# Two small powers on GpSimd behind every second row transfer of the scatters

## The chip, the cores and the metric

The kernel runs on one core of one Trainium2 chip. The metric is the device time of one execution in microseconds (us): the median of three runs before the change is 1126.06 us (1124.15 to 1128.71).

## The reference

Eight sequences of 512 tokens of 128 values pass through two layers. Each layer is an attention and a feed-forward part with experts, each behind a layer norm and with a residual.

```python
x = x + _L0_attn_ref(_layernorm(x), ...)   # 16 heads of 8, 4 key/value heads, causal
x = x + _L0_ffn_ref(_layernorm(x), ...)    # 8 experts, the best one a token, silu(a) * g @ w2
x = x + _L1_attn_ref(_layernorm(x), ...)   # keys and values from a latent of 32, rotary positions, causal
x = x + _L1_ffn_ref(_layernorm(x), ...)    # 8 experts, the best two a token, relu(x w1 + b1) w2 + b2
```

## The kernel before

**Attention.** The work goes batch by batch (8 batches of 512 tokens) through both layers. For each batch TensorE first makes scores for the row maxima, in units of up to 512 columns by two banks (L1354, L1360), and VectorE reduces them (`neg_max`, L1658). GpSimd computes the lowest part of the split maxima (`max_parts`, L1220), SyncE stores it and loads it back into the query stack (L1079, L1085). Then TensorE makes the transposed scores (L1380), ScalarE the exponentials (`scratch`, L1588), GpSimd sets the part above the diagonal to zero (`affine_select` on `scratch`, L1230, four a quad of heads), and TensorE multiplies with the values (`psum<-scratch,values`, L1398), which ScalarE copies out (`ctx_raw`, L1484). GpSimd has further small steps: four operations of the layer norm's statistics with one power (L1185 to L1190), the lowest parts of queries and keys (L1207), sums of the rotary products (L1212, L1216).

**Experts.** After four batches (a half, g = 0 or 1) VectorE chooses experts for 2048 tokens and computes, for each token, its row in a list sorted by expert (`rows_of`, L1866). GpSimd then scatters the normed rows (`xn_half`) to these places in device memory (`sorted_in`, L1241): one indirect DMA moves 128 rows, 16 of them a half in layer 0, and 2 x 16 a half in layer 1, where the second 16 (k = 1) of a batch wait for a mark that VectorE writes into the rows (`xn_half`, L1677) once the first 4 of the batch have landed. SyncE fetches the sorted rows in groups of four tiles (`rows_in`, L1130), the first group of a half once all scatters of the half have landed, and the weights of each tile's expert (`w_now`, L1116). TensorE transposes the rows (L1449) and computes the two products of each tile of 128 rows (L1466, L1476), with ScalarE (L1624) and VectorE (L1655) between. In layer 0 the results go to memory and come back by indirect gathers (L1258). In layer 1 GpSimd sends each tile back with an indirect DMA (`returned`, L1249), and SyncE takes the rows back at the end (L1150).

**Order.** Every engine has one fixed program. A table of times (`schedule`) gives each step a due time, and `Plan` walks it with costs per step and makes one order for each engine (`plan.order`). Attention of later batches and experts of a half are interleaved in these orders. An engine doesn't pass a step that waits. On GpSimd the scatters are steps of their own; those of layer 0 stand in one row, those of layer 1, half 0, stand among masks of the attention, and those of layer 1, half 1, stand among sends. Each waits only at its batch's first transfer:

```python
elif s.kind == "scatter":
    g, x, (t, k) = s.b, s.x, s.y
    if t == QT * x and k == 0:
        pool.wait_ge(placed, s.layer * HALVES + g + 1)
        pool.wait_ge(normed, of("norm", s.layer, g * GB + x, "half").n + 1)
        pool.wait_ge(filled[s.layer], FILLED[s.layer])
    if t == QT * x and k == 1:
        pool.wait_ge(marked, of("mark", 1, g, x).n + 1)
```

Of the kernel before, what the change touches and what calls it, by code (L numbers as in the profile page):

```python
# [8 lines left out]
ALU = mybir.AluOpType  # L9
# [5 lines left out]
QT = SEQ // P  # L15
# [48 lines left out]
C_ID, C_FIRST, C_ONE, C_RANK, C_THR, C_SLOT, C_HALF = 0, 128, 256, 264, 272, 288, 328  # L64
C_TOKEN = 332
C_EPS, C_MINUS = C_TOKEN + GT, C_TOKEN + GT + QT
# [37 lines left out]

TAKE_BEHIND = 14
DMA = 16

ROW = DIM + 1
RETURNED = 2 * GT * P
# [625 lines left out]
def two_layers(nc, d):  # L735
    with ExitStack() as ctx:
# [3 lines left out]
        def sem(name):  # L740
            return ctx.enter_context(nc.semaphore(name))
# [8 lines left out]
        consts = sb("consts", [P, C_ALL])  # L750
# [58 lines left out]
        r_small = sb("route_small", [P, 4, GT])  # L809
# [43 lines left out]
        route_exp, normed = sem("route_exp"), sem("normed")  # L853

        values_set, zeroed, lat_made = sem("values_set"), sem("zeroed"), sem("lat_made")
        rs_made, stats_made = sem("rs_made"), sem("stats_made")
        lat_scaled, lo_made, summed, max_lo, masked = sem("lat_scaled"), sem("lo_made"), sem("summed"), sem("max_lo"), sem("masked")

        rows_set = sems("rows_set", STACKS)
# [12 lines left out]

        REST_LOADED = REST_LOADS * DMA
        W2_LOADED = EXPERTS * DMA
        FILLED = [len(times) * DMA for times in FILLS]

# [15 lines left out]
        def parks_done(s):  # L892

            done = 0
            for k in range(stack_of(s), batch_of(s) + 1, STACKS):
                done += DMA * 3
            return done

        def stacks_done(name, k):

            return sum(4 * DMA if name == "k" and j < BATCHES else 2 * DMA for j in range(k % STACKS, k + 1, STACKS))

# [35 lines left out]
        def rows_sent(layer, g, x):  # L938

            return DMA * QT * (g + 1) if layer == 0 else DMA * QT * (HALVES + 2 * (g + 1))  # L940

# [228 lines left out]
        @block.gpsimd  # L1170
        def _(pool):
            for i in range(3):
                pool.memset(values[i][:, :, :], 0.0).then_inc(values_set, 1)
            for i in range(3):
                pool.wait_ge(values_set, 3)
                pool.memset(values_of(i, HEADS)[:, :, :, HD:VW], 1.0).then_inc(values_set, 1)
            pool.memset(gathered[0], 0.0).then_inc(zeroed, 1)
            pool.wait_ge(consts_loaded, 2 * DMA)
            for s in plan.order("pool"):
                if s.kind == "stats":  # L1180

                    mean, var, scale, shift = (ln_small[s.slot][:, :, x:x + 1] for x in range(6, 10))
                    pool.wait_ge(var_made, s.n + 1)
                    eps, half, minus = (consts[:, x:x + QT].unsqueeze(2) for x in (C_EPS, C_HALF, C_MINUS))
                    pool.tensor_tensor(scale, var, eps, ALU.add).then_inc(rs_made, 1)  # L1185
                    pool.tensor_tensor(shift, mean, minus, ALU.mult).then_inc(rs_made, 1)
                    pool.wait_ge(rs_made, 3 * s.n + 2)
                    pool.tensor_tensor(scale, scale, half, ALU.pow).then_inc(rs_made, 1)  # L1188
                    pool.wait_ge(rs_made, 3 * s.n + 3)
                    pool.tensor_tensor(shift, shift, scale, ALU.mult).then_inc(stats_made, 1)  # L1190

                elif s.kind == "norm":

                    b = s.b
                    out = lat_n[:, :, :]
                    pool.wait_ge(normed, s.n + 1)
                    pool.tensor_tensor(out, out, ln_gb[:, 0:1, :].to_broadcast([P, QT, LATENT]), ALU.mult).then_inc(lat_scaled, 1)
                    pool.wait_ge(lat_scaled, b + 1)
                    twice = [P, QT, 2, LATENT]
                    pool.tensor_tensor(lat_twice[:, :, :, :], out.unsqueeze(2).to_broadcast(twice), ln_gb[:, 1:2, :].unsqueeze(1).to_broadcast(twice),  # L1200
                                       ALU.add).then_inc(lat_made, 1)

                elif s.kind == "mid":
                    n = P if s.layer == 0 and s.x == "k" else SEQ
                    pool.wait_ge(mid_made, s.n + 1)
                    parts, rest = parts_of[s.x], rest_of[s.layer, s.x]
                    pool.tensor_tensor(parts[:, 2, 0:n], rest[:, 0:n], parts[:, 1, 0:n], ALU.subtract).then_inc(lo_made, 1)  # L1207

                elif s.kind == "sum":
                    u = (of("rotate", 1, s.b, "q", 1) if s.x == "q" else of("rotate_k", 1, s.b)).uses[0]  # L1210
                    pool.wait_ge(read[u.bank], u.after)
                    pool.tensor_tensor(exact[:, :], rot[0][:, :], rot[1][:, :], ALU.add).then_inc(summed, 1)  # L1212

                elif s.kind == "hi":
                    pool.wait_ge(hi_made, 2 * batch_of(s) + (s.x == "k") + 1)
                    pool.tensor_tensor(rest_of[1, s.x][:, :], exact[:, :], parts_of[s.x][:, 0, :], ALU.subtract).then_inc(rest_made, 1)  # L1216

                elif s.kind == "m_mid":
                    pool.wait_ge(max_mid, s.n + 1)
                    pool.tensor_tensor(max_parts[:, 2, :], max_rest[:, :], max_parts[:, 1, :], ALU.subtract).then_inc(max_lo, 1)  # L1220

                elif s.kind == "score":

                    u = s.uses[0]
                    pool.wait_ge(read[u.bank], u.after)
                    units, stride, offs = MASKS[s.y]
                    first = 2 * SEQ * (s.slot - units + 1)
                    for off in offs:
                        diag = scratch[:, first:first + 4 * stride].rearrange("p (x n) -> p x n", x=4)[:, :, off:off + P]
                        pool.affine_select(out=diag, in_=diag, compare_op=ALU.is_ge, fill=0.0, base=0, pattern=[[0, 4], [1, P]],  # L1230
                                           channel_multiplier=-1).then_inc(masked, 1)
# [8 lines that stand above are left out]
                        pool.wait_ge(marked, of("mark", 1, g, x).n + 1)  # L1240
                    pool.indirect_dma_start(sorted_in[s.layer][g][:, :], bass.IndirectOffsetOnAxis(ap=rows_of[g][k][:, t:t + 1], axis=0),  # L1241
                                            xn_half[:, t, 0:widths[s.layer]], None).then_inc(scattered[x], DMA)

                elif s.kind == "send":
                    g, slot = s.b, of("second", 1, s.b, s.x).slot
                    u = of("second", 1, g, s.x).uses[0]
                    pool.wait_ge(places_known, places_read(of("turn_rows", 1, g, s.x // 4)))
                    pool.wait_ge(read[u.bank], u.after)
                    pool.indirect_dma_start(returned[g][:, :], bass.IndirectOffsetOnAxis(ap=goes_to[g][:, s.x:s.x + 1], axis=0),  # L1249
                                            kept[slot], None).then_inc(sent_back[slot], DMA)  # L1250

                elif s.kind == "combine":
                    g, x, (t, k) = s.b, s.x, s.y
                    if t == QT * x and k == 0:
                        for slot, value in enumerate(stores_made(g)):
                            pool.wait_ge(stored[slot], value)
                    if s.n >= 4:
                        pool.wait_ge(combined, s.n - 3)  # L1258
                    pool.indirect_dma_start(gathered[s.slot], None, sorted_out[g][:, :],
                                            bass.IndirectOffsetOnAxis(ap=rows_of[g][k][:, t:t + 1], axis=0)).then_inc(gathered_in[s.slot], DMA)  # L1260

                elif s.kind == "add":
                    rows = X[:, s.b * GT + QT * s.x:s.b * GT + QT * s.x + QT, :]
                    pool.wait_ge(weighed, s.y + 1)
                    if s.y:
                        pool.wait_ge(added_apart, s.y)
                    pool.tensor_tensor(rows, rows, taken_back(s.b, s.x, s.y), ALU.add).then_inc(added_apart, 1)
# [706 lines left out]
```

## Time and profile before

| | |
|---|---|
| median of the timed runs | 1126.06 us |
| span of the profiled execution, first to last instruction | 1133.8 us |
| mean granted TensorE clock | 0.890 |
| TensorE busy | 920.3 us, 81% |
| VectorE busy | 649.8 us, 57% |
| ScalarE busy | 611.0 us, 54% |
| GpSimd busy | 516.6 us, 46% |
| scatters L1241 | 96, 92.7 us, mean 966 ns |
| sends L1249 | 78, 75.4 us, mean 966 ns |
| masks L1230 | 256, 159.4 us, mean 639 ns |
| powers of the statistics L1188 | 40, 41.2 us, mean 1030 ns |

The profile is of one execution. Its span, 1133.8 us, is what the page gives as that execution's own time; what lies around the span is not in it. Busy shares are means over stages that differ. An idle time is put down to the releaser that came last; "issue" is time in which the engine waited for nothing that the profile shows, and "remote" (in the chain "another core or an unknown queue") a wait whose end the trace can't put down to any engine. PEclk is the share of full clock that was granted to TensorE. Lines are those of the kernel before; a helper's line (L1655, L1658, L1484) serves many steps.

### The profile page before, as it was taken

The page shows a single profiled execution, that of the slowest core. Times are in us where ns is not written, and L with a number is a line of the kernel's source. Part 1 is how long each engine was busy: PE and PEld are TensorE (multiplying, and loading weights), DVE is VectorE, ACT ScalarE, POOL GpSimd, SP SyncE. Part 2 cuts the span into 40 slices and gives each one's busy share as a digit, 9 for nine tenths or more (in the row PEclk, how much of TensorE's full clock was granted, in tenths as well). Part 3 has the DMA queues.
Part 4 walks back from the last instruction along what each step waited for, and adds up shares of the span by engine and source line. Part 5 has one row for each costly group of instructions (what it writes and reads, how often), then busy time and mean ns, then how long its engine had stood idle before and what let it go on. Part 6 is the DMA issues. An engine that isn't in the chain of part 4 may idle for free.

```text
span 1133.8 us, 24903 instructions
## 1 busy us (share of the span) xinstructions
PE 920.3 (81%) x8964; PEld 605.2 (53%) x8964; DVE 649.8 (57%) x1266; ACT 611.0 (54%) x1170; POOL 516.6 (46%) x747
## 2 busy tenths in 40 slices
PE   4789889848998899975999789987689984788781
PEld 2344445415986445432897345533245774687771
DVE  1987988838434787785556787887455151011116
ACT  3277777702454766853544478763368752254451
POOL 3153443460013875556103775647744436615452
PEclk9999999967999887996999899996769996898896
DMA  6446233252763251452762445334311454466657
GB/s 165 109 126 182 66 88 74 74 158 60 231 204 105 73 149 70 89 155 63 219 200 87 91 139 136 88 86 138 80 37 33 127 150 119 141 184 174 174 160 233
DMA packets 136722, 142.75 MB, mean 126 GB/s; under 512 B 35036, under 2 KB 112924, under 8 KB 136444
## 3 DMA queue, kind: packets, MB, share of 16 engines
q1 hardware_dynamic: 130012, 127.61, 40.9%
q0 software_dynamic: 6592, 13.55, 3.7%
q8 instruction: 76, 1.25, 0.5%
q14 instruction: 42, 0.34, 0.1%
HBM read 100.32 MB, written 45.95 MB: 129 GB/s over the span
## 4 chain that ended last, share of the span: by engine, by line
PE 57%; DVE 12%; ACT 10%; another core or an unknown queue 9%; issue 6%; DMA 3%; POOL 2%; SPq 1%; DVEq 0%; ACTq 0%; POOLq 0%
PE psum L1466 13%; PE psum L1398 12%; PE psum L1476 9%; DVE neg_max L1658 8%; PE psum L1380 5%; ACT scratch L1588 5%; PE psum L1354 5%; PE psum L1424 2%; PE psum L1360 2%; ACT hidden_t L1624 2%; PE psum L1433 1%; PE psum L1286 1%; PE psum L1316 1%; PE psum L1408 1%
## 5 line engine op out<-in xcount | busy, mean ns | idle before, releaser
L1658 DVE TENSOR_REDUCE neg_max<-psum 128x2 f32<-128x768 f32 (+3 forms) x352 | 381.1, 1119 | 117.1 <-PE psum L1360 69.6
L1588 ACT ACTIVATE scratch<-psum 128x1024 f32<-128x1024 f32 x320 | 317.3, 1023 | 128.6 <-PE psum L1380 85.2
L1230 POOL TENSOR_SCALAR_AFFINE_SELECT scratch<-scratch 128x512 f32<-128x512 f32 x256 | 159.4, 639 | 309.1 <-ACT scratch L1588 308.5
L1398 PE MATMUL psum<-scratch,values 128*32 128x512 f32 (+3 forms) x2048 | 180.8, 479 | 3.5 <-POOL scratch L1230 3.0
L1354 PE MATMUL psum<-k_stack,q_stack 52*128 52x128 bf16 (+3 forms) x1024 | 140.3, 335 | 51.2 <-DVE neg_max L1658 23.7
L1466 PE MATMUL psum<-rows_t,w_now 128*128 128x128 f32 x1360 | 179.1, 284 | 1.9 <-issue 1.3
L1466 PEld LDWEIGHTS psum<-rows_t,w_now 128*128 128x128 f32 x1360 | 166.4, 198 | 9.0 <-issue 6.4
L1476 PE MATMUL psum<-w,hidden_t 128*128 x992 | 142.2, 290 | 34.7 <-ACT hidden_t L1624 19.8
L1380 PE MATMUL psum<-q_stack,k_stack 55*128 55x512 bf16 (+3 forms) x1024 | 129.0, 324 | 47.7 <-DVE neg_max L1658 19.1
L1476 PEld LDWEIGHTS psum<-w,hidden_t 128*128 128x128 f32 x992 | 127.8, 202 | 44.8 <-issue 44.6
L1624 ACT ACTIVATE hidden_t<-psum,w_now 128x128 f32<-128x128 f32 x312 | 88.0, 371 | 104.0 <-PE psum L1466 50.5
L1655 DVE TENSOR_TENSOR w<-psum,w_now 128x128 f32<-128x128 f32 x78 | 22.6, 293 | 184.9 <-PE psum L1476 108.6
L1249 POOL DMA_INDIRECT returned<-w,goes_to x78 | 75.4, 966 | 96.1 <-DVE w L1655 50.9
L1354 PEld LDWEIGHTS psum<-k_stack,q_stack 52*128 52x128 bf16 x1024 | 44.9, 100 | 134.2 <-issue 53.6
L1241 POOL DMA_INDIRECT sorted_in<-xn_half,rows_of x96 | 92.7, 966 | 42.0 <-issue 25.6
L1360 PE MATMUL psum<-masks_bf 64*128 64x64 bf16 (+2 forms) x1408 | 97.0, 218 | 1.0 <-issue 1.0
L1380 PEld LDWEIGHTS psum<-q_stack,k_stack 55*128 55x128 bf16 x1024 | 37.7, 97 | 110.6 <-issue 52.6
L1398 PEld LDWEIGHTS psum<-scratch,values 128*32 128x32 f32 x2048 | 57.7, 116 | 72.2 <-issue 49.1
L1360 PEld LDWEIGHTS psum<-masks_bf 64*128 64x128 bf16 x1408 | 73.6, 104 | 34.6 <-issue 10.9
L1885 DVE SCALAR_TENSOR_TENSOR hidden_t<-w,psum 128x512 f32<-128x512 f32 x46 | 31.6, 687 | 69.3 <-PE psum L1466 42.0
L1484 ACT ACTIVATE ctx_raw<-psum 128x512 f32<-128x512 f32 x32 | 19.1, 598 | 92.1 <-PE psum L1398 74.5
L1188 POOL TENSOR_TENSOR ln_small<-ln_small,consts 128x4 f32<-128x4 f32 x40 | 41.2, 1030 | 3.1
(123 smaller groups left out, 966.9 us busy)
## 6 DMA issues: line engine op xcount, KB each, us to landing
w_now<-in_w SPq DMA_DIRECT2D x78, 322.0 KB
w_now<-in_w SPq DMA_DIRECT2D x46, 512.0 KB
q_stack<-q_parts SPq DMA_DIRECT2D x64, 192.0 KB
q_parts<-q_parts SPq DMA_DIRECT2D x16, 384.0 KB, 3.9
k_stack<-k_parts SPq DMA_DIRECT2D x32, 192.0 KB, 3.4
rows_in<-sorted_in SPq DMA_DIRECT2D x18, 258.0 KB
sorted_in<-in_empty_rows SPq DMA_DIRECT2D x8, 516.0 KB
q_parts<-q_parts SPq DMA_DIRECT2D x16, 256.0 KB, 3.3
```

The source lines that it names most:

```text
L1230: pool.affine_select(out=diag, in_=diag, compare_op=ALU.is_ge, fill=0.0, base=0, pattern=[[0, 4], [1, P]], channel_multiplier=-1).then_inc ...
L1241: pool.indirect_dma_start(sorted_in[s.layer][g][:, :], bass.IndirectOffsetOnAxis(ap=rows_of[g][k][:, t:t + 1], axis=0), xn_half[:, t, 0:wi ...
L1249: pool.indirect_dma_start(returned[g][:, :], bass.IndirectOffsetOnAxis(ap=goes_to[g][:, s.x:s.x + 1], axis=0), kept[slot], None).then_inc( ...
L1354: pe.matmul(out[:, j * width:(j + 1) * width], q_stack[i][rows, pair, t * P:(t + 1) * P], k_stack[i][rows, k_of(layer, pair), 0:width], st ...
L1360: ins = pe.matmul(blocks, ident_of[half, :], mask[half, :].unsqueeze(1).to_broadcast([P // 2, n, P // 2]), start=False, stop=(first > widt ...
L1380: ins = pe.matmul(bank[u.bank + k][:, off:off + SEQ - j * P], k_stack[i][rows, k_of(layer, pair), j * P:(j + 1) * P], q_stack[i][rows, pai ...
L1398: ins = pe.matmul(bank[u.bank][CW * c:CW * c + CW, j * P:SEQ], values[batch_of(s) % 3][:, j, col:col + CW], p[:, c % 2, off:off + SEQ - j ...
L1466: ins = pe.matmul(bank[v.bank][:, c * P:(c + 1) * P], w1_now[layer][w.slot][:, n * FFN + c * P:n * FFN + (c + 1) * P], rows)
L1476: ins = pe.matmul(bank[u.bank][:, 0:P], hidden_t[h.slot][:, k * P:(k + 1) * P], w2[layer][:, bass.ds(e, 1), k * DIM:(k + 1) * DIM].rearran ...
L1588: act.activation(expd[s.slot], psum[:, u.bank:u.bank + 2, :], ACT.Exp, scale=SCALE).then_inc(read[u.bank], 1)
L1624: ins = act.activation(hidden_t[s.slot][:, c * P:(c + 1) * P], bank[u.bank][:, c * P:(c + 1) * P], ACT.Relu, bias=w[:, FFN + c:FFN + c + 1])
L1658: return dve.tensor_reduce(out=out, in_=in_, axis=AX, op=op, negate=negate)
```

## The change

Behind each scatter with an odd tile number t, GpSimd computes the same power twice: four values of `eps` to the power of four values of -1/2, from the constants, into an unused row of `route_small`. The second and every later power wait for the semaphore that the one before raised. Nobody reads the result.

```diff
+PAUSE = 2
...
-        rs_made, stats_made = sem("rs_made"), sem("stats_made")
+        rs_made, stats_made, paused = sem("rs_made"), sem("stats_made"), sem("paused")
...
             pool.wait_ge(consts_loaded, 2 * DMA)
+            pauses = [0]
+
+            def pause():
+
+                for n in range(PAUSE):
+                    if pauses[0]:
+                        pool.wait_ge(paused, pauses[0])
+                    pool.tensor_tensor(r_small[:, 2, 0:QT], consts[:, C_EPS:C_EPS + QT], consts[:, C_HALF:C_HALF + QT], ALU.pow).then_inc(paused, 1)
+                    pauses[0] += 1
+
             for s in plan.order("pool"):
...
                                             xn_half[:, t, 0:widths[s.layer]], None).then_inc(scattered[x], DMA)
+                    if t % 2:
+                        pause()
```

The orders of the engines stay as they were; only the powers come in. The mask and the small subtraction behind the scatters stand as follows: GpSimd in layer 0, half 0, before (L1241 are the scatters, L1220 the maxima's lowest part, L1230 a mask):

```order
L1230 AFFINE_SELECT scratch<-scratch 128x4x128 x2
L1241 DMA sorted_in<-xn_half,rows_of 2944x128 x16
L1220 TENSOR_TENSOR max_parts<-max_rest,max_parts 32x128
L1230 AFFINE_SELECT scratch<-scratch 128x4x128
L1207 TENSOR_TENSOR k_parts<-rot,k_parts 128x128
```

And now, the start and the end of the same stretch (lines are those of the changed kernel: L1253 the scatters, L1188 the powers of the pause, L1232 the maxima's lowest part, L1242 a mask):

```order
L1242 AFFINE_SELECT scratch<-scratch 128x4x128 x2
L1253 DMA sorted_in<-xn_half,rows_of 2944x128 x2
L1188 TENSOR_TENSOR route_small<-consts 128x4 x2
L1253 DMA sorted_in<-xn_half,rows_of 2944x128 x2
```

Between these rows and the next, scatters and powers alternate by twos in the same way. The end of the stretch:

```order
L1253 DMA sorted_in<-xn_half,rows_of 2944x128 x2
L1188 TENSOR_TENSOR route_small<-consts 128x4 x2
L1232 TENSOR_TENSOR max_parts<-max_rest,max_parts 32x128
L1242 AFFINE_SELECT scratch<-scratch 128x4x128
L1219 TENSOR_TENSOR k_parts<-rot,k_parts 128x128
```

Eight pauses stand between the first scatter and the mask, the last of them behind the last scatter. GpSimd in layer 1, half 0, from the 18th scatter on, before:

```order
L1241 DMA sorted_in<-xn_half,rows_of 4992x129 x2
L1230 AFFINE_SELECT scratch<-scratch 128x4x128 x3
L1241 DMA sorted_in<-xn_half,rows_of 4992x129 x7
L1230 AFFINE_SELECT scratch<-scratch 128x4x128
L1241 DMA sorted_in<-xn_half,rows_of 4992x129
L1230 AFFINE_SELECT scratch<-scratch 128x4x128 x3
```

And now, from the 20th scatter to the 28th:

```order
L1253 DMA sorted_in<-xn_half,rows_of 4992x129
L1188 TENSOR_TENSOR route_small<-consts 128x4 x2
L1253 DMA sorted_in<-xn_half,rows_of 4992x129 x2
L1188 TENSOR_TENSOR route_small<-consts 128x4 x2
L1253 DMA sorted_in<-xn_half,rows_of 4992x129 x2
L1188 TENSOR_TENSOR route_small<-consts 128x4 x2
L1253 DMA sorted_in<-xn_half,rows_of 4992x129 x2
L1188 TENSOR_TENSOR route_small<-consts 128x4 x2
L1242 AFFINE_SELECT scratch<-scratch 128x4x128
L1253 DMA sorted_in<-xn_half,rows_of 4992x129
L1242 AFFINE_SELECT scratch<-scratch 128x4x128 x3
L1253 DMA sorted_in<-xn_half,rows_of 4992x129
```

Four pauses stand here between the 20th and the 27th scatter, in the place of none; the masks keep their places among the scatters.

## Rows read from the trace of the kernel before

**Rows 1.** Page: busy time of the engines, then the chain's shares by engine.

```profile
PE 920.3 (81%) x8964; PEld 605.2 (53%) x8964; DVE 649.8 (57%) x1266; ACT 611.0 (54%) x1170; POOL 516.6 (46%) x747
...
PE 57%; DVE 12%; ACT 10%; another core or an unknown queue 9%; issue 6%; DMA 3%; POOL 2%; SPq 1%; DVEq 0%; ACTq 0%; POOLq 0%
```

**Rows 2.** Windows: stretch, length, busy (x count) by engine, PEclk, DMA share, GB/s.

```profile
229.90:251.30 21.40, 8.89 (x80) 4.51 (x72) 4.62 (x8) 1.33 (x2) 16.51 (x18) 0.66 0.58 175
...
845.00:882.00 37.00, 34.70 (x402) 19.83 (x400) 20.09 (x36) 30.69 (x50) 12.91 (x23) 1.00 0.17 42
...
1070.00:1114.00 44.00, 35.00 (x267) 32.53 (x267) 10.12 (x39) 20.36 (x70) 22.45 (x23) 0.95 0.64 188
```

**Rows 3.** Timeline, GpSimd, first scatters: start, us, line, operation [idle, releaser].

```profile
231.34 0.96 POOL L1241 DMA_INDIRECT sorted_in<-xn_half,rows_of  x1 [0.30 <-issue]
...
249.01 0.96 POOL L1241 DMA_INDIRECT sorted_in<-xn_half,rows_of  x1 [0.30 <-issue]
...
250.37 0.64 POOL L1230 TENSOR_SCALAR_AFFINE_SELECT scratch<-scratch 128x512 f32<-128x512 f32 x1
```

**Rows 4.** Timeline, the other engines and SyncE's queue, in the same stretch.

```profile
238.50 0.96 DVE L1658 TENSOR_REDUCE neg_max<-psum 128x2 f32<-128x768 f32 x1 [4.87 <-remote]
...
251.33 0.94 SPq L1130 DMA_DIRECT2D rows_in<-sorted_in  x2
...
252.68 15.72 DVE L1658 TENSOR_REDUCE neg_max<-psum 128x2 f32<-128x768 f32 x15 [13.22 <-remote]
...
265.71 2.79 PE L1398 MATMUL psum<-scratch,values 128*32 128x384 f32 x24
```

**Rows 5.** Timeline near the end, where GpSimd sends rows back.

```profile
1080.88 0.96 POOL L1249 DMA_INDIRECT returned<-w,goes_to  x1 [0.30 <-issue]
...
1082.65 2.17 ACT L1624 ACTIVATE hidden_t<-psum,w_now 128x128 f32<-128x128 f32 x8 [2.82 <-remote]
...
1083.99 0.96 POOL L1249 DMA_INDIRECT returned<-w,goes_to  x1 [2.15 <-DVE goes_to L1669]
```

**Rows 6.** Timeline, GpSimd: a power, what depends on it; a scatter behind a mask.

```profile
278.50 1.04 POOL L1188 TENSOR_TENSOR ln_small<-ln_small,consts 128x4 f32<-128x4 f32 x1
279.63 0.20 POOL L1190 TENSOR_TENSOR ln_small<-ln_small 128x4 f32<-128x4 f32 x1
...
843.84 1.03 POOL L1241 DMA_INDIRECT sorted_in<-xn_half,rows_of  x1 [0.17 <-issue]
```

**Rows 7.** Timeline, layer 0, half 1: mask behind the scatters, then values.

```profile
519.91 0.65 POOL L1230 TENSOR_SCALAR_AFFINE_SELECT scratch<-scratch 128x512 f32<-128x512 f32 x1
...
533.50 1.06 PE L1398 MATMUL psum<-scratch,values 128*32 128x512 f32 x8
```

**Rows 8.** Waits, 765.7 to 843.8 (us, times, longest), and timeline: layer 1, half 0.

```profile
POOL scratch L1230 <- ACT scratch L1588: 16.7, 7, 5.7
...
765.70 1.07 POOL L1241 DMA_INDIRECT sorted_in<-xn_half,rows_of  x1 [1.26 <-DVE rows_of L1866]
...
843.03 0.64 POOL L1230 TENSOR_SCALAR_AFFINE_SELECT scratch<-scratch 128x512 f32<-128x512 f32 x1 [2.04 <-ACT scratch L1588]
...
845.46 1.50 PE L1398 MATMUL psum<-scratch,values 128*32 128x384 f32 x24
```

**Rows 9.** Waits, 935 to 990, and timeline: layer 1, half 1.

```profile
POOL sorted_in L1241 <- DVE xn_half L1677: 10.0, 3, 5.8
...
935.88 0.96 POOL L1241 DMA_INDIRECT sorted_in<-xn_half,rows_of  x1 [2.43 <-DVE rows_of L1866]
...
984.08 0.96 POOL L1241 DMA_INDIRECT sorted_in<-xn_half,rows_of  x1 [0.30 <-issue]
...
1002.79 0.93 SPq L1130 DMA_DIRECT2D rows_in<-sorted_in  x2
...
1007.49 0.66 PE L1449 MATMUL psum<-consts,rows_in 128*128 128x128 f32 x4 [0.18 <-DMA rows_in<-sorted_in]
...
1013.25 0.95 POOL L1249 DMA_INDIRECT returned<-w,goes_to  x1 [21.90 <-DVE goes_to L1669]
```

## The prediction

> **What bounds the kernel now.** I read the page's busy times and chain first. TensorE is busy for 81% of a span of 1133.8 us and makes 57% of the chain [rows 1], so a stretch in which TensorE idles is paid for unless it idled there anyway. The windows show where it idles [rows 2]. In the 21.4 us of the first scatters (layer 0, half 0) it is busy 8.9 us and ScalarE 1.3 us, at a granted clock of 0.66; right behind the scatters of layer 1, half 0, it is busy 34.7 of 37 us at full clock.
>
> The timeline says why. GpSimd issues its 16 scatters back to back, one each 1.26 us ((249.01 - 231.34) / 14), and its next mask comes at 250.37 [rows 3]. Meanwhile the others don't merely wait for GpSimd: VectorE's maximum at 238.50 had waited 4.87 us and the one at 252.68 13.22 us, both for "remote", which is nothing that the trace knows, and SyncE's next fetch is issued at 251.33, 1.36 us behind the end of the last scatter [rows 4]. I read this as a **freeze**: while the software queue is kept full, waits on all the other engines end late, and they end about a microsecond or two after the last transfer was issued. It shows on a small scale behind three transfers back to back: the third ends at 1081.84, ScalarE starts at 1082.65 after 2.82 us of "remote" [rows 5]. Yet there, where transfers come in twos and threes with some 2 us between, TensorE is busy 35.0 of 44 us [rows 2, 5]. So a pause behind every second scatter should let the others go on at some 80%. That is what the change can win. What it can lose is the time on GpSimd itself, which works in order and has the causal masks and the small subtractions behind the scatters.
>
> **What is added.** 96 scatters, a pause behind each odd one: 48 pauses, 96 powers. Nothing is removed and nothing changes place. The same power of 128x4 in the statistics takes 1.04 us, and what depends on it starts 1.13 us behind its start. A pause is 1.13 + 1.04, plus 0.17 us to the next transfer (as behind a mask), less the 0.30 us that stood between two transfers [rows 6]: 2.04, with 0.02 us to start it **2.06 us**. In all 98.9 us of GpSimd's time: 8 pauses (16.5 us) in each half of layer 0, 16 (33.0 us) in each half of layer 1. What of it reaches the end is read at the next step that TensorE needs.
>
> - Layer 0, half 0. The mask at 250.37 ends at 251.01; now at 267.5. TensorE's values (L1398) that read it start at 265.71 before [rows 4], so 14.7 of 16.5 us lie under work that stands ahead of them: 15 maxima on VectorE, which the freeze had pushed behind the scatters and which now run in the pauses. **+1.8 us.** If they don't run there, all 16.5.
> - Layer 0, half 1. The first mask behind the scatters ends at 520.56; now at 537.1. The values that read it start at 533.50 before [rows 7]. **+3.6 us.**
> - Layer 1, half 0. The 32 scatters lie among masks (the order is shown above). From the first scatter at 765.70 to the end of the mask at 843.67 GpSimd waits 16.7 us for ScalarE's exponentials [rows 8]. 15 pauses lie ahead of that mask: 30.9 us. If the thawed ScalarE is always ahead, these waits vanish, and the mask ends at 843.67 - 16.7 + 30.9 = 857.9. TensorE reads it at 845.46 [rows 8]: **+12.4 us**, and nothing gives them back, since the 37 us behind are full [rows 2]. If every wait stays, it is 29.1 us. I take 1.7 us for waits that stay, near the low end, since the longest of them (5.7 us) is one that a thaw should take away whole, and each of the others is shorter than the pauses that GpSimd has made by then: **+14.1 us.**
> - Layer 1, half 1. Scatters run from 935.88 to 985.04, with 10.0 us of waits for the marks on VectorE [rows 9], which sit behind frozen expert steps. Paused, the first 16 take 36.7 us, so the marks are all there, and the last of the second 16 ends 34.3 us later, at 1006.9. The first rows of this half are fetched at 1002.79 before, now at 1006.9 + 1.4 = 1008.3: **+5.5 us** on TensorE's transposes at 1007.49 [rows 9]. Before, 17.8 us lay between the last scatter and that fetch, which hung on TensorE's experts of half 0; now it hangs on the scatters. The sends behind the scatters move by 22 us, but GpSimd idled 21.9 us behind them before the first send of this half [rows 9], so they hold up nobody.
>
> Sum: 1.8 + 3.6 + 14.1 + 5.5 = **25.0 us**. The profiled execution would go from 1133.8 to 1158.8 us; its span is 7.7 us above the median of the timed runs, 1126.06, which I take to be the profiler's own, so the forecast is 1126.06 + 25.0 = **1151 us**, 2.2% slower. The bounds of the terms: 0 where the gates are met earlier than the rows say, 16.5 + 16.5 + 29.1 + 15 = 77 where half of the thaw fails everywhere. Added work on VectorE and TensorE: none. The powers write an unused row of a small tile and read constants, so nobody waits for them; the next thing on GpSimd does.
>
> One rule speaks against the thaw. The trace shows ScalarE, TensorE and VectorE held up while only GpSimd and the queues work [rows 2, 4]. The Trainium skill (SBUF — State Buffer, section "Who interferes with whom") says that the port pair of VectorE and GpSimd is the only point of contention between engines, and that "PE and ACT never wait on anyone". By that rule there would be nothing for a pause to free; it would be the second rival below, 1223 us. The trace disagrees with it as far as ScalarE's 1.3 busy us in 21.4 show.
>
> **The rivals.**
> 1. Half a thaw (1177 us). The masks of layer 1, half 0, keep GpSimd waiting as before (29.1 instead of 14.1 us), and the marks of half 1 still take their 10.0 us: 1151 + 15 + 10 = 1176, rounded up by the clock that idle stretches cost. For it: with transfers in twos and threes "remote" waits of near 3 us still occur [rows 5]. Against: marks and maxima have 16 us and more of pauses to run in.
> 2. No thaw, the freeze lasts through the pauses (1223 us). Data still on the way when the next pair is issued keeps everyone frozen: 16.5 + 16.5 + 30.9 + 33.0 = 96.9. For it: thaw comes 0.8 to 2.7 us after the last issue, and a pause is 2.1. Against: 80% busy in the last window of [rows 2].
> 3. Faster (1113 us). The freeze is dearer than it looks and the gates cheaper. Place: the four scatter stages. Price: TensorE idles 12.5 us in the first [rows 2], some 50 us in four of the kind; it also runs at 0.66 clock there. If half comes back (25 us) and the gates hold for half of what I count (12 us), it is 1126 - 25 + 12. It decides from the point at which the mask behind the scatters is wanted later than it is made: 267.5 against 265.71 is close in the first stage, where 2 us turn the sign; it is far off in layer 1, where GpSimd has 92 us of work for 78 us.
> 4. No change (1126 us): the thaw pays for the gates exactly, or idle time of TensorE further on (19% of the span) swallows 25 us.
>
> **How the numbers follow.** A measurement of this kernel can tell about 0.5% from no change, 5.6 us. Chances: forecast (1138 to 1166) 0.56, half a thaw (1166 to 1195) 0.18, no thaw 0.07, faster 0.11, no change 0.08. Slower than 1131.7: 0.56 + 0.18 + 0.07 = 0.81; within 0.5%: 0.08; faster 0.11. The range leaves out no thaw and faster, 0.18 together: from 1126 - 1 to the upper end of half a thaw, less its far tail: 1125 to 1188.
>
> **What would show it.** In the profile after: 96 powers of about 1.03 us, pairs of scatters each 4.58 us, GpSimd's busy time up by some 98 us. In the first scatter stage TensorE busier than 8.9 us per 21.4 us and no "remote" wait above 5 us, with VectorE's maxima inside the stage; the values behind it at +1.8 us, waiting for GpSimd's mask. In layer 1, half 0, GpSimd's waits for exponentials near nil and TensorE behind by 12 to 14 us. The first fetch of half 1 waiting for scatters and not for an expert. Wrong would be: "remote" waits of 13 us inside paused stages (rival 2), or TensorE reaching the steps behind each stage earlier than before (rival 3).

## The result, and the profile after

The changed kernel takes 1162.18 us, median of 4 runs (1159.9 to 1164.18); the kernel before, timed beside it, 1125.11 us (1122.08 to 1128.71). The ratio is 1.032, with a 95% interval from 1.029 to 1.034: slower, by 37 us. The forecast was 1151 us with a range from 1125 to 1188. The profiled execution has a span of 1159.2 us where the forecast for it was 1158.8: from profile to profile the change costs 25.4 us, and from median to median 37.

The page of the changed kernel, against [rows 1]: busy time of the engines, then the shares of the chain by engine, then the group of the added powers.

```profile
PE 918.0 (79%) x8964; PEld 598.1 (52%) x8964; DVE 648.7 (56%) x1266; ACT 612.1 (53%) x1170; POOL 619.0 (53%) x843
...
PE 46%; POOL 21%; DVE 10%; ACT 8%; issue 7%; DMA 4%; another core or an unknown queue 2%; SPq 1%; POOLq 0%; DVEq 0%; ACTq 0%
...
L1188 POOL TENSOR_TENSOR route_small<-consts 128x4 f32<-128x4 f32 x96 | 98.5, 1026 | 4.9
```

GpSimd's busy time is up by 102.4 us, of which the 96 powers are 98.5. In the chain GpSimd goes from 2% to 21%, and "another core or an unknown queue" from 9% to 2%. One kind of wait has been exchanged for the other.

The windows, columns as in [rows 2]. The first scatter is issued at 233.03 now. The first row is 21.4 us from there, as the first of [rows 2] was from its first scatter; the second is the whole stage, from 233.0 to 268.0:

```profile
233.03:254.43 21.40, 14.19 (x162) 6.69 (x154) 20.29 (x23) 1.33 (x2) 18.72 (x19) 0.66 0.52 154
233.00:268.00 35.00, 14.22 (x162) 6.69 (x154) 20.31 (x23) 1.33 (x2) 30.54 (x31) 0.60 0.35 106
```

VectorE is busy 20.3 of 21.4 us where it was busy 4.6, and TensorE 14.2 where it was busy 8.9. Its maxima, which had waited 13.22 us for "remote" [rows 4], are now one unbroken group that starts inside the stage. The timelines of VectorE, GpSimd, SyncE's queue and TensorE there:

```profile
233.86 19.65 DVE L1672 TENSOR_REDUCE neg_max<-psum 128x4 f32<-128x1024 f32 x19
...
266.94 0.96 POOL L1253 DMA_INDIRECT sorted_in<-xn_half,rows_of  x1 [0.30 <-issue]
267.91 2.13 POOL L1188 TENSOR_TENSOR route_small<-consts 128x4 f32<-128x4 f32 x2
...
270.39 0.63 POOL L1242 TENSOR_SCALAR_AFFINE_SELECT scratch<-scratch 128x512 f32<-128x512 f32 x1
...
270.96 0.94 SPq L1132 DMA_DIRECT2D rows_in<-sorted_in  x2
...
271.07 2.79 PE L1412 MATMUL psum<-scratch,values 128*32 128x384 f32 x24 [20.18 <-POOL scratch L1242]
```

These are the same products with the values as in [rows 4] (L1398 before, L1412 now). TensorE has stood idle for 20.18 us ahead of them, and what ended its wait is GpSimd's mask. The other three stages, at the rows that answer to [rows 7], [rows 8] and [rows 9]; TensorE, and for the last one SyncE's queue ahead of it:

```profile
539.09 1.93 PE L1412 MATMUL psum<-scratch,values 128*32 128x512 f32 x8 [18.69 <-POOL scratch L1242]
...
866.10 2.36 PE L1412 MATMUL psum<-scratch,values 128*32 128x384 f32 x16
...
1030.67 0.93 SPq L1132 DMA_DIRECT2D rows_in<-sorted_in  x2
...
1033.65 1.97 PE L1463 MATMUL psum<-consts,rows_in 128*128 128x128 f32 x8 [19.88 <-DMA rows_in<-sorted_in]
```

The waits for "remote" add up to 199.0 us in the whole trace of before, 149.8 of them in the four scatter stages (22.6, 24.7, 31.5 and 71.0). In the changed kernel they are 56.9 us, and in the four stages there is none. Of the rest, 12.5 us lie between the scatter stages, and 44.4 behind 1030, where GpSimd sends rows back and the change has put no pause. These are the waits from 1060 on (us, times, longest):

```profile
DVE w L1669 <- remote: 29.0, 7, 5.4
ACT hidden_t L1638 <- remote: 9.2, 4, 3.0
ACT rows_t L1498 <- remote: 2.0, 2, 1.7
```

**What comes late.** The packed traces also hold the time of every recorded update of a semaphore, which no view prints; what follows is worked out from them. Each of the waits for "remote" is for a semaphore that TensorE raises, and that update stands in the trace 1.5 to 18.1 us behind the end of the last matmul that raises it. VectorE's maximum at 252.68 waits for a matmul that ended at 234.61, and the update is recorded at 252.66, though TensorE ran other matmuls until 248.7. In the kernel run again (below) the same maximum waits for a matmul that ended at 238.19, and the update stands at 238.21. Ahead of the last matmul of the program, 70 of TensorE's updates are over 1 us late in the trace of before, 30 in that of the changed kernel, none of them in its four scatter stages, and none in the kernel run again; those of VectorE, ScalarE and GpSimd are late in no trace of these. So what the prediction calls a freeze is a late signal from TensorE to those who wait for it, and not a halt of all engines.

### The profile page after: what moved, and what is told of

Same layout as the page of the kernel before. It is cut to its first block, busy times and chain, and to the rows that moved or that the text cites. A ratio compares the mean times of both kernels' runs of the same rounds, so it can differ in the third digit from the quotient of the medians.

```text
span 1159.2 us, 24999 instructions
## 1 busy us (share of the span) xinstructions
PE 918.0 (79%) x8964; PEld 598.1 (52%) x8964; DVE 648.7 (56%) x1266; ACT 612.1 (53%) x1170; POOL 619.0 (53%) x843
## 4 chain that ended last, share of the span: by engine, by line
PE 46%; POOL 21%; DVE 10%; ACT 8%; issue 7%; DMA 4%; another core or an unknown queue 2%; SPq 1%; POOLq 0%; DVEq 0%; ACTq 0%
PE psum L1480 11%; PE psum L1412 10%; POOL route_small L1188 8%; POOL sorted_in L1253 8%; PE psum L1490 8%; DVE neg_max L1672 5%; ACT scratch L1602 4%; PE psum L1394 4%; PE psum L1368 4%; POOL scratch L1242 2%; PE psum L1374 1%; POOL w L1273 1%; PE psum L1438 1%; DVE X L1700 1%
## 5 line engine op out<-in xcount | busy, mean ns | idle before, releaser
L1242 POOL TENSOR_SCALAR_AFFINE_SELECT scratch<-scratch 128x512 f32<-128x512 f32 x256 | 159.9, 642 | 289.2 <-ACT scratch L1602 288.6
L1412 PE MATMUL psum<-scratch,values 128*32 128x512 f32 (+3 forms) x2048 | 186.9, 492 | 62.4 <-POOL scratch L1242 61.8
L1490 PE MATMUL psum<-w,hidden_t 128*128 x992 | 139.2, 286 | 26.8 <-DVE w L1669 18.9
L1490 PEld LDWEIGHTS psum<-w,hidden_t 128*128 128x128 f32 x992 | 124.2, 197 | 37.2 <-issue 36.8
L1412 PEld LDWEIGHTS psum<-scratch,values 128*32 128x32 f32 x2048 | 58.7, 118 | 135.1 <-POOL scratch L1242 70.2
L1253 POOL DMA_INDIRECT sorted_in<-xn_half,rows_of x96 | 96.2, 1002 | 27.8 <-issue 21.5
L1188 POOL TENSOR_TENSOR route_small<-consts 128x4 f32<-128x4 f32 x96 | 98.5, 1026 | 4.9
L1374 PEld LDWEIGHTS psum<-masks_bf 64*128 64x128 bf16 x1408 | 73.4, 104 | 34.4 <-issue 11.1
L1394 PEld LDWEIGHTS psum<-q_stack,k_stack 55*128 55x128 bf16 x1024 | 37.4, 97 | 90.5 <-issue 38.4
L1498 ACT ACTIVATE ctx_raw<-psum 128x512 f32<-128x512 f32 x32 | 19.1, 598 | 101.3 <-PE psum L1412 92.0
L1899 DVE SCALAR_TENSOR_TENSOR hidden_t<-w,psum 128x512 f32<-128x512 f32 x46 | 31.6, 686 | 68.9 <-PE psum L1480 42.4
```

What stands on the lines that cost most here:

```text
L1188: pool.tensor_tensor(r_small[:, 2, 0:QT], consts[:, C_EPS:C_EPS + QT], consts[:, C_HALF:C_HALF + QT], ALU.pow).then_inc(paused, 1)
L1374: ins = pe.matmul(blocks, ident_of[half, :], mask[half, :].unsqueeze(1).to_broadcast([P // 2, n, P // 2]), start=False, stop=(first > widt ...
L1394: ins = pe.matmul(bank[u.bank + k][:, off:off + SEQ - j * P], k_stack[i][rows, k_of(layer, pair), j * P:(j + 1) * P], q_stack[i][rows, pai ...
L1412: ins = pe.matmul(bank[u.bank][CW * c:CW * c + CW, j * P:SEQ], values[batch_of(s) % 3][:, j, col:col + CW], p[:, c % 2, off:off + SEQ - j ...
L1490: ins = pe.matmul(bank[u.bank][:, 0:P], hidden_t[h.slot][:, k * P:(k + 1) * P], w2[layer][:, bass.ds(e, 1), k * DIM:(k + 1) * DIM].rearran ...
```

## The experiments

I first meant to learn what each stage pays and whether a shorter pause is enough. The first batch changed the question, because one of its kernels was the kernel before, unchanged.

**The kernel before, again.** No edit.

> The kernel before, profiled once more and timed against itself. Theory A (the freeze during back-to-back scatters is there in every execution and alike): ratio 1.000, span of the profile 1133 to 1135 us, first scatter to the values behind it 35.8 us as in the first profile. Theory B (the profiled execution of the kernel before was a slow one, and the freeze varies from run to run): span of the profile 1120 to 1128, ratio 1.000, and the 8 to 11 us that are missing show in shorter scatter stages.

Measured: 1044.06 us, and the same for the runs of before beside it (ratio 1.000, 0.997 to 1.003), 81 us less than where the first runs were made. From profile to profile the difference is 93 us (spans of 1133.8 and 1040.8). Each batch ran on a chip of its own, four in all; which one the first runs had isn't recorded. I call theirs the first chip, and the batches' the second to the fifth, though the first may be one of these at another hour. The scatters have the same rhythm. These are the rows of its trace: the windows of the first stage and one of its length that begins at the first scatter here; VectorE; GpSimd; TensorE; SyncE's queue.

```profile
229.90:251.30 21.40, 16.51 (x172) 7.63 (x172) 20.11 (x29) 2.18 (x3) 15.88 (x17) 0.66 0.54 177
232.50:253.90 21.40, 15.00 (x166) 7.10 (x162) 20.34 (x23) 1.33 (x2) 16.55 (x18) 0.66 0.54 176
...
238.23 15.73 DVE L1658 TENSOR_REDUCE neg_max<-psum 128x2 f32<-128x768 f32 x15 [0.43 <-PE psum L1360]
...
251.69 0.96 POOL L1241 DMA_INDIRECT sorted_in<-xn_half,rows_of  x1 [0.30 <-issue]
252.67 0.44 POOL L1220 TENSOR_TENSOR max_parts<-max_rest,max_parts 32x128 bf16<-32x128 f32 x1
253.05 0.64 POOL L1230 TENSOR_SCALAR_AFFINE_SELECT scratch<-scratch 128x512 f32<-128x512 f32 x1
...
253.74 2.79 PE L1398 MATMUL psum<-scratch,values 128*32 128x384 f32 x24 [2.41 <-POOL scratch L1230]
...
254.01 0.94 SPq L1130 DMA_DIRECT2D rows_in<-sorted_in  x2
```

The same 16 transfers go out back to back, and nothing is frozen: VectorE is busy 20.34 us of 21.40, its 15 maxima run behind a wait of 0.43 us instead of 13.22, and no wait of this trace is for "remote". TensorE's values follow the mask at once. What I had read as the effect of a full software queue is thus seen with it on one chip, or in one condition of a chip, and doesn't come from the kernel alone. One of my signs was none: SyncE's fetch comes 1.36 us behind the end of the last scatter here too (254.01 - 252.65), without a freeze.

**A part of the change at a time**, in the same batch, with the same 1044 us beside them. The expectations still take the freeze for given, and what they forecast for it misses in all three.

One power for two:

```diff
-PAUSE = 2
+PAUSE = 1
```

> The change with one power a pause instead of two: a pause of some 1.0 us. Thaw-and-gates theory (the others run in the pauses, GpSimd's own work sets the gates): layer 0, half 0, mask at 259, under the 265.7 at which it was wanted; GpSimd has 77 us of work for 78 in layer 1, half 0; the fetch of layer 1, half 1, comes at about 994 instead of 1003. So the gates cost 0 to 2 us and what was frozen comes back: 1105 to 1128 us against 1125, and 35 to 55 us less than the change. No-thaw theory (pauses only add GpSimd time and the freeze lasts): half of the change's loss stays, 1140 to 1147 us.

Measured: 1086.66 us, ratio 1.041 (1.038 to 1.044), +42.6 us.

Layer 0 alone:

```diff
-                    if t % 2:
+                    if t % 2 and s.layer == 0:
```

> The change with pauses in layer 0 alone. Thaw-and-gates theory by the two profiles: the gates of layer 0 cost +2.2 and +4.0 us from the first scatter to the values, so 1128 to 1133 us (+3 to +8). If the 11 us by which the loss was larger in the timed runs than between the two profiles come from layer 0: +12 to +17 us, 1137 to 1142. No thaw: +33 us, 1158.

Measured: 1082.54 us, ratio 1.035 (1.030 to 1.041), +38.5 us.

Layer 1, half 0, alone:

```diff
-                    if t % 2:
+                    if t % 2 and (s.layer, g) == (1, 0):
```

> The change with pauses in layer 1, half 0, alone, where scatters lie among masks. Thaw-and-gates theory: the largest term, +14 us, 1137 to 1142 us. If masks that come late cost nothing since TensorE catches up: under +5 us.

Measured: 1076.55 us, ratio 1.031 (1.028 to 1.034), +32.5 us.

One power in each pause costs somewhat less than half of what two will cost (42.6 us, and 98.6 below). The 16 pauses of layer 0 cost more than their 33 us of GpSimd, the 16 of layer 1, half 0, just that. Where nothing is frozen there is nothing to thaw, and the pauses are paid whole. From this, the change as a whole was forecast for a chip of this kind, and the missing stage run by itself, in a second batch on a third chip (before: 1042.78 us).

**The change itself, there.**

> The change itself, on the chip of this batch. Where the kernel before takes some 1044 us (no freeze): each stage pays its pauses nearly whole, as the kernels with a part of them did: 38 (layer 0) + 32 (layer 1, half 0) + 25 to 33 (layer 1, half 1) = 95 to 103 us, so 1139 to 1147 us, a ratio of 1.09 to 1.10; values behind the first scatters some 17 us later than before and waiting for GpSimd's mask alone. Where before takes some 1125 us (freeze): 1160 to 1164 us, a ratio of 1.03, and the maxima of VectorE inside the stage only with the pauses. If the freeze were not what made the pauses cheap on the first chip, the ratio would be 1.03 on both.

Measured: 1141.42 us (1138.22 to 1145.89), ratio 1.094 (1.088 to 1.100), +98.6 us, at the forecast made for it. The ratio of 1.03 belongs to the first chip.

**Layer 1, half 1, alone.**

```diff
-                    if t % 2:
+                    if t % 2 and (s.layer, g) == (1, 1):
```

> Pauses in layer 1, half 1, alone: 16 pauses, 33 us of GpSimd. Forecast as on record: +5.5 us, for the stage before ends 17.8 us before its first fetch. Without a freeze the scatters end nearer to that fetch: the scatters there last 49 us in the first trace, with 10 us of waits for marks that pauses would cover, so +15 to +30 us, 1059 to 1074 us beside a before of 1044. If the cost is in the layers' later use of GpSimd (the sends) and not in the fetch, the fetch does not move.

Measured: 1073.36 us, ratio 1.028 (1.023 to 1.032), +30.6 us, the upper end of what was expected. The parts add up to 38.5 + 32.5 + 30.6 = 101.6 us, the whole is 98.6.

How much each stage costs can be read off by setting each matmul's start beside the start of the same matmul in the kernel run again (all traces have 8964, in one order but for six at most). This table is worked out from the traces; us later (+) than there. The columns are eight times of the kernel run again, counted as in its profile. They stand at the start of each stage and behind it: 235 and 265, 488 and 519, 732 and 854, then 854 and 946 for the fourth. The last is the start of the last matmul:

```
                                     235     265     488     519     732     854     946    1018
before, first traces                -2.8   +12.1   +13.4   +28.5   +28.9   +42.9   +69.0   +92.5
changed, first traces               +0.3   +18.0   +16.2   +35.3   +35.5   +65.4   +97.0  +117.9
changed, third chip                 -4.1   +13.6   +14.2   +33.3   +34.7   +64.4   +95.5   +97.7
layer 0 alone                       -3.7   +14.0   +14.6   +33.6   +35.8   +36.9   +37.1   +39.8
layer 1, half 0, alone              +0.1    +0.8    -2.1    +1.0    +1.1   +33.8   +34.2   +36.9
layer 1, half 1, alone              -2.6    -1.8    -7.4    -3.1    -0.7    +0.5   +31.7   +34.3
```

Three things stand in it. First, the freeze cost the kernel before 15.0 us in the first stage (-2.8 to +12.1), 15.1 in the second, 14.0 in the third, 26.1 in the fourth and 23.4 behind it (differences are taken before rounding). Second, in the four stages the changed kernel pays the same on the frozen chip (17.7, 19.1, 30.0, 31.6) as on the third chip (17.7, 19.1, 29.7, 31.0), within 0.6 us: with the pauses, next to nothing of the freeze is left there. The thaw is complete, but the pause costs more than it frees. Third, the differences of the two rows of the first traces stand beside the terms of the prediction (1.8, 3.6, 14.1, 5.5): 17.7 - 15.0 = 2.7, 19.1 - 15.1 = 4.0, 30.0 - 14.0 = 16.0 and 31.6 - 26.1 = 5.5.

Behind the scatters, where the rows are sent back, the changed kernel of the first traces loses what the third chip doesn't: +20.9 against +2.2 us from 946 to the end. From the first row sent back on there are no pauses, and there its 44.4 us of waits for "remote" lie.

**The powers in bunches.** Four behind every fourth scatter.

```diff
-                    if t % 2:
-                        pause()
+                    if t % QT == QT - 1:
+                        for n in range(QT // 2):
+                            pause()
```

> The same 96 powers, four of them behind every fourth scatter where the change has two behind every second. The same time of GpSimd to every mask behind a stage. Without a freeze the place of the powers within a stage does not matter: the same time as the change within 0.5%. With a freeze a run of four scatters (5 us) freezes the others longer, but the pause behind it (4.3 us) is also longer: 0 to +10 us against the change. If thaw costs a fixed time at each pause, bunching would be faster than the change by up to 10 us.

Measured, in the batch of the change itself: 1136.22 us (1132.23 to 1137.75), ratio 1.087 (1.082 to 1.093). In layer 0 its matmuls stand within 0.5 us of those of the change (+13.9 at 265, +33.4 at 519); the 3 us between the profiles arise in layer 1. The intervals of the two ratios overlap, so a difference is unclear. Bunched, the powers still cost 93 us, so the cost doesn't hang on where in a stage they stand; that is what to expect where only GpSimd's time counts. How bunches thaw wasn't seen.

**The masks ahead.** To see whether GpSimd's order is what passes the time on, I moved its steps in the kernel before. No pauses.

```diff
+EARLY = (2, 1)
+EARLY_AT = (6, 8)
...
-            for s in plan.order("pool"):
+            steps = list(plan.order("pool"))
+            for g in range(2):
+                at = [i for i, s in enumerate(steps) if s.kind == "scatter" and (s.layer, s.b) == (0, g)]
+                moved = steps[at[-1] + 1:at[-1] + 1 + EARLY[g]]
...
+                del steps[at[-1] + 1:at[-1] + 1 + EARLY[g]]
+                steps[at[0] + EARLY_AT[g]:at[0] + EARLY_AT[g]] = moved
+            for s in steps:
```

> No pauses. Of the kernel before, GpSimd's first small subtraction and first mask behind the scatters of layer 0, half 0, stand behind the sixth of them, and the first mask of half 1 behind the eighth. Theory that GpSimd's place in line is what costs: without a freeze TensorE waits 2.4 us for the first and 0.6 us for the second, so -2 to -3 us (1041 to 1042 beside 1044), and 3.9 us are lost nowhere since the rows are fetched 1 us later only. With a freeze: TensorE's values wait for maxima behind the scatters anyway, 0 to -3 us. Theory that scatters in one unbroken run are what costs: a mask of 0.64 us in the middle breaks the run and some 2 to 8 us come back with a freeze.

Measured: 1041.26 us beside 1042.78, ratio 0.999 (0.995 to 1.002): within what a measurement can tell. In the trace the wait of 2.41 us is gone and the stage is 2.6 us shorter (from -3.2 at 235 to -5.8 at 265, in the terms of the table); nothing is gained in half 1. The mechanism shows, but it is too small to make a better kernel here.

**Both: pauses in layer 0 and masks ahead.** The diffs of layer 0 alone and of the masks ahead, together, in a batch with 1044.77 us beside it.

> The pauses of layer 0 alone (as in the kernel that cost 38 us on the second chip), with the masks moved ahead as in the kernel before it: the first subtraction and mask of half 0 behind the sixth scatter, the first mask of half 1 behind the eighth. If only the mask behind the scatters passes a pause on to TensorE, as the prediction had it, its values are free of the pauses and the 38 us fall to 10 or less (1044 + 10 = 1054 us). If the whole of what stands behind the scatters does (the rows' fetch, which the scatters' own end releases, the next subtraction, the statistics), TensorE's values start near 253 and it then waits at the transposes of the fetched rows, which come at 270 + 1.4 + 3.1 = 274.5 as in the change: 30 to 38 us stay (1073 to 1081 us). Where before takes 1125 us (freeze), the same comparison by the places at which TensorE waits.

Measured: 1075.63 us, ratio 1.031 (1.024 to 1.038), +30.9 us, in the lower end of the second theory's 30 to 38. TensorE, in the first stage, and SyncE's queue ahead of the wait:

```profile
250.09 2.79 PE L1421 MATMUL psum<-scratch,values 128*32 128x384 f32 x24
...
269.56 0.94 SPq L1134 DMA_DIRECT2D rows_in<-sorted_in  x2
...
272.57 1.97 PE L1472 MATMUL psum<-consts,rows_in 128*128 128x128 f32 x8 [14.94 <-DMA rows_in<-sorted_in]
```

The values are free of the pauses: they start at 250.09. Then TensorE idles 14.94 us for the rows which the scatters bring and SyncE fetches. From 235 to 265 this trace loses 14.8 us (-0.7 to +14.2), where layer 0 alone, without the moved masks, lost 17.7: the moved masks save about the 2.6 us that they save without pauses, and no more. So the mask is only the first of two gates that stand at nearly the same place: the fetch, which comes 1.35 us behind the end of the last scatter (268.21), is the other. In the changed kernel the fetch stands 3.06 us behind that end (270.96 - 267.90), for SyncE first stores the lowest parts of the maxima (270.45), which GpSimd computes behind the last pause. The first theory, that the mask alone passes the pause on, falls.

**One power, once more.**

> The kernel with one power in each pause once more, one look, to find a chip with the freeze. Where before takes some 1044 us: 1085 to 1089 us again. Where before takes some 1125 us (freeze): a pause of 1.0 us ends as the first held-up waits end (0.8 us behind the last issue), so if it thaws as the pause of two powers does, 1162 less some 50 us, 1105 to 1128 us, faster than before or the same; if it is too short to thaw, 1165 to 1180 us with waits of 5 us and more of no known releaser inside the stages.

Measured: one timed run of each, 1086.59 us beside 1040.72, on a fifth chip: no freeze. So the kernel before was timed in four batches on four chips, each time at 1041 to 1045 us. Whether one power would have thawed as well as two is therefore open: it could only be tried where the freeze is.

## Why the prediction was right, and where it was not

**The reading of the freeze** (waits end late while GpSimd issues transfers back to back, and a pause lets the engines go on) holds for the chip of the first traces in what it forecasts. Shown by the maxima inside the stage, by waits for "remote" that fall from 149.8 us to none in the four stages, and by the table, where the paused stages cost the same with and without a freeze. Read too widely was "waits on all the other engines": late are TensorE's signals alone, and the others stand still for want of them. I had counted with 80% of full work in the pauses; it was nearly all of it in the four stages. Rivals 1 and 2, the incomplete thaws, fall with that.

**Layer 0, half 0: +1.8 forecast.** The profile gives +2.2 from the first scatter to the values (271.07 - 233.03 against 265.71 - 229.88). That the 15 maxima hide most of the 16.5 us was right. The maxima are 15.7 us here, and the freeze had cost 15.0. The gate was read too narrowly, though: I named the mask alone, and the run with both edits shows TensorE waiting for the rows' fetch at nearly the same time.

**Layer 0, half 1: +3.6.** +4.0 by the same sum (539.09 - 501.51 against 533.50 - 499.88, the first scatters of the two traces).

**Layer 1, half 0: +14.1.** The values go from 79.76 us behind the first scatter to 93.9 us (866.10 less 772.24, the first scatter after), +14.1. GpSimd's idle time for exponentials in the stage, between those places, was 16.7 us and is 0.2 now. That the term came out to the tenth is partly luck: I had left 1.7 us of these waits, 1.5 too many, but a pair of scatters with its pause takes 4.63 us and not 4.58, 0.75 too few over 15 pauses, and the other 0.7 us I haven't traced. The cost doesn't arise at the last mask, as the term reads, but all through the stage. TensorE's waits for masks and for ScalarE's norm, which itself had waited 9.0 us for GpSimd's statistics (us, times, longest):

```profile
PE psum L1412 <- POOL scratch L1242: 18.5, 6, 5.4
...
PE psum L1300 <- ACT xn_half L1561: 4.4, 1, 4.4
```

**Layer 1, half 1: +5.5.** +6.4 at the fetch (1030.67 - 957.37 against 1002.79 - 935.88). It waits for the scatters now and TensorE for it, as forecast.

The four are 26.7 us against 25.0. Between the stages some us come and go (+3.15 ahead of the first scatter, where nothing was changed, -3.7 between the halves of layer 0, +1.8 between the later stages, -2.5 behind the last fetch), -1.3 together: 25.4.

**The step that failed** is the base: "its span is 7.7 us above the median, which I take to be the profiler's own". In the changed kernel the profiled execution has a span of 1159.2 us and a time of 1161.48, and the timed runs have the same; in the kernel run again it is 1040.8 and 1042.78. So the profiler adds nothing that these runs show. With the 2.3 us around its span the profiled execution of before took 1136.1 us, which is 7.4 above the slowest of the timed runs and 11 above their median: it was an execution slower than those. So 25 us from profile to profile became 37 between medians, and that is why 1162 and not 1151 came out. Set on the profile's own time, the sum would have given 1133.8 + 25.0 + 2.3 = 1161. What slowed that one execution isn't known, and so the terms, whose sizes were taken from it, account for 25 of the 37 us, and it is the width of the range that took in the rest. Where the other 12 lie can't be said without the trace of a typical run of before on that chip.

**What I took for a property of the program** is one of the place it ran. I also said that the trace disagrees with the Trainium skill (SBUF — State Buffer, "Who interferes with whom"), by which only the port pair of VectorE and GpSimd causes contention and TensorE and ScalarE never wait on anyone. It doesn't show that. The section speaks of the ports to SBUF, and ScalarE's waits for "remote" in the trace of before (4.5 us in the first stage, 11.1 in the second) are waits for a late signal from TensorE; no run here shows TensorE or ScalarE held up at a port. ScalarE's 1.33 busy us in the first stage are just as few in the kernel run again, for want of work rather than by a freeze, so my citing them as the evidence was wrong; VectorE's maxima were the evidence. Rival 2, no gain from a thaw, at 96.9 us, is what the change does where there was no freeze: +98.6 us, for another reason than the rival gave.

**Rival 3, faster**, had the thaw right and lost on the gates: GpSimd works in order, and what TensorE needs next stood behind the scatters and their pauses in three stages, and among them in layer 1, half 0. The thaw gave back some 15 us in each half of layer 0, and the pauses took 16.9 us of GpSimd's own time there (from the first scatter to the mask 37.4 us, after 20.5 in the kernel run again).

Not settled: why TensorE's signals come late. Nothing in the traces names a cause, and the freeze came in none of four later batches. A condition of one chip fits; so does one of that hour. That back-to-back transfers bring the lateness on there is argued from where it begins and ends, and from the stages with pauses, which have none.

## What to carry to other kernels

A pause on an engine that works in order costs its whole length at whatever stands behind it, unless that has slack: before adding one, find every consumer of that line, the mask and the transfers' own end alike, and read how late each is wanted. A wait whose releaser the trace can't name may belong to the place of the run and not to the program; look first at when the work that it waits for had ended, and time the unchanged kernel on another chip before tuning against it. And ask whether the profiled execution is a typical one before laying its distance from the timed runs to the profiler.

## What the runs showed of the hardware

- The same program took 1125 us in the first runs and 1041 to 1045 us in four later batches, each on a chip of its own. The difference is in waits on VectorE and ScalarE for signals of TensorE, and through them on TensorE (199.0 us of waits for "remote" in all, the longest 13.22). In the first trace 70 updates of TensorE's semaphores are over 1 us late, up to 18.1 us; in the kernel run again none are, and half of them come within 0.02 us of the matmul's end.
- The late signals stand in and around runs of back-to-back row transfers from GpSimd: scatters, and gathers and sends too (at 630.60 behind gathers, at 922.09 behind sends). The transfers themselves go out at 1.26 us each with and without them. Pauses of 2.1 us behind every second transfer came with the end of all such waits in the four paused stages; 56.9 us remained in the rest of the kernel.
- TensorE's granted clock in the 21.4 us from the first scatter is 0.66 in the frozen trace, in the free one and in the paused one alike (TensorE busy 8.89, 15.00 and 14.19 us). So the low clock there did not come from the freeze.
- A power of 128x4 takes 1.03 us; two behind each other 2.13, four 4.32. The scatter behind a power takes 1.03 us, one behind another scatter 0.96.
